# A nine-step scan on four engines: a bias and half of a multiply moved to ScalarE

## What is computed

```python
def mmnorm(x):
    return x / (jnp.max(jnp.abs(x), axis=-1, keepdims=True) + EPS)
def _scanner(y, x, freq_W, freq_b, out_W, out_b):
    z = jnp.concatenate([y, x], axis=-1)
    f = z @ freq_W + freq_b
    z = jnp.concatenate([jnp.sin(f), jnp.cos(f)], -1) @ out_W + out_b
    return mmnorm(z)
qv = x @ attn_W + attn_b
q, v = (qv[..., :c], qv[..., c:])
n = 1
while n < t:
    prev = jnp.concatenate([jnp.broadcast_to(identity, (b, n, c)), q[:, :t - n]], axis=1)
    q = _scanner(prev, q, freq_W, freq_b, out_W, out_b)
    n *= 2
Y = q * v
return Y @ proj_W + proj_b
```

## Time and profile before

| | |
|---|---|
| median of three runs | 2502.61 us (2501.95 to 2506.33) |
| profiled execution | 2498.18 us, span 2496.5 us |
| granted TensorE clock, mean | 0.983 of full |
| busy: TensorE, VectorE, ScalarE, GpSimd | 90%, 77%, 44%, 3% of the span |
| the scan's rounds | from about 66 to 475 us of the span |

### The profile page before, as it was taken

How to read it: one execution, slowest core, us unless ns; L and a number is a source line. 1 busy time by engine, 2 the same in 40 slices (tenths; PEclk the granted TensorE clock), 3 DMA queues, 4 the chain that set the end, 5 groups by cost and what they waited for, 6 DMA issues and landing times. The chain is left out here.

```text
span 2496.5 us, 37786 instructions
## 1 busy us (share of the span) xinstructions
PE 2254.8 (90%) x12609; PEld 1590.9 (64%) x12609; DVE 1923.8 (77%) x5516; ACT 1089.9 (44%) x1481; POOL 82.9 (3%) x135
## 2 busy tenths in 40 slices
PE   5999999899999998999879998998998999999997
PEld 4777777667666676676534454445675676666765
DVE  5768676689888889889845554555898898898897
ACT  1334343343443443544435554553444434434433
POOL 3200000000000000000000000000000000000000
PEclk9999999999999999999989998998999999999999
DMA  7000000000000000000000000000000000000000
GB/s 203 1 1 0 0 0 1 1 1 1 1 0 1 0 0 1 0 1 1 1 1 1 1 1 1 1 1 1 1 9 9 0 9 9 0 9 0 9 9 9
DMA packets 20782, 18.35 MB, mean 7 GB/s; under 512 B 6555, under 2 KB 19871, under 8 KB 20648
## 3 DMA queue, kind: packets, MB, share of 16 engines
q1 hardware_dynamic: 16106, 14.04, 1.9%
q10 hardware_dynamic: 4542, 2.78, 0.4%
HBM read 12.60 MB, written 4.19 MB: 7 GB/s over the span
## 5 line engine op out<-in xcount | busy, mean ns | idle before, releaser
L1355 ACT ACTIVATE f_E<-f_two 128x1024 f32<-128x1024 f32 x256 | 248.1, 1021 | 324.4 <-PE f_two L1237 324.4
L1091 DVE SCALAR_TENSOR_TENSOR f_E<-f_two,f_E 128x1024 f32<-128x1024 f32 x256 | 312.5, 1221 | 72.1 <-ACT f_E L1355 64.1
L1227 PE MATMUL f_acc<-ue,f_mid 128*128 128x256 f32 x1024 | 254.7, 395 | 11.7 <-DVE f_mid L1076 11.5
L1227 PEld LDWEIGHTS f_acc<-ue,f_mid 128*128 128x128 f32 x1024 | 192.9, 195 | 54.8 <-DVE f_mid L1076 18.6
L1142 PE MATMUL f_two<-f_hT,wg 128*128 128x512 f32 x768 | 211.4, 410 | 10.9 <-DVE f_mid L960 10.9
L1325 ACT ACTIVATE f_gate<-f_two,bg 128x512 f32<-128x512 f32 x128 | 88.1, 688 | 271.2 <-PE f_two L1142 270.9
L1142 PE MATMUL f_two<-f_hT,wu 128*128 128x512 f32 x768 | 200.0, 395 | 0.0
L1803 ACT ACTIVATE b_U<-b_two 128x768 f32<-128x768 f32 (+1 forms) x192 | 160.7, 886 | 69.2 <-PE b_two L1673 68.8
L1184 PE MATMUL f_acc<-wd,f_mid 128*128 128x256 f32 x768 | 188.1, 388 | 0.0
L1142 PE MATMUL f_two<-f_hT,deT 128*128 128x512 f32 x768 | 184.4, 395 | 0.0
L1142 PEld LDWEIGHTS f_two<-f_hT,wg 128*128 128x128 f32 x768 | 142.3, 188 | 49.8 <-DVE f_mid L960 15.3
(11 more groups left out here) (258 smaller groups left out, 3961.1 us busy)
## 6 DMA issues: line engine op xcount, KB each, us to landing
x<-in_L_attn_a_x SPq DMA_DIRECT2D x8, 512.0 KB, 7.4
out_x<-x SPq DMA_DIRECT2D x8, 512.0 KB, 2.9
de_rows<-in_L_ffn_down_embed ACTq DMA_DIRECT2D x1, 1024.0 KB, 5.8
wd<-in_L_ffn_Wd SPq DMA_DIRECT2D x1, 1024.0 KB, 10.1
ue<-in_L_ffn_up_embed SPq DMA_DIRECT2D x16, 64.0 KB, 5.8
whole_g<-in_L_ffn_Wg SPq DMA_DIRECT2D x1, 1024.0 KB, 6.3
whole_u<-in_L_ffn_Wu SPq DMA_DIRECT2D x1, 1024.0 KB, 8.8
ffq<-in_L_ffn_Wq ACTq DMA_DIRECT2D x4, 128.0 KB, 9.2
```

What stands on the lines that cost most here:

```text
L1091: dve.scalar_tensor_tensor(out=two_heads, in0=wide(turns, ("R", u))[:], scalar=PICKED_ABOVE, in1=two_heads, op0=ALU.is_gt, op1=ALU.mult).t ...
L1227: mm = pe.matmul(acc[:, j * C:(j + 1) * C], mixed[c % 2][:, j * P:(j + 1) * P], w.ue[:, c, :], start=False, stop=True, skip_group_check=True)
L1355: act.activation(E[:, c % 2, 2 * p:2 * p + 2].rearrange("p h t -> p (h t)"), wide(turns, ("S", u))[:], ACT.Exp).then_inc(S.act_read, 1)
```

## The change

It has two parts.

1. In steps 0 to 7, `gs` of lane 0 is written once and not twice by VectorE: 512 elements. ScalarE then copies the first place to the second, at the end of its step, behind the column writes, and sets `dup_ready`, for which TensorE's features of lane 0 wait in steps 1 to 8. Lane 1 is as before.
2. In steps 1 to 7 TensorE's `gain_bias(1, "gz")` is gone. ScalarE writes the bias into gb1 as 512 elements from `bias_gz`, a broadcast row of 128 columns, between whole0 and wave0. It waits there for lane 1's `gs_ready` (gb1 has been read) and sets `g1_begun`, for which TensorE waits between the zb product and the gb product of lane 1. Step 0 keeps TensorE's bias. The set-up gets one product and one ScalarE copy that make `bias_gz`.

```diff
+        bias_gz = ctx.enter_context(nc.sbuf_tensor("a_bias_gz", [P, P], F32))
...
                                 dve.wait_ge(S.g_psum, nth(i, NS, s + 1, l) + START)
-                                by = spread(spread(scale[l][:].rearrange("p j q -> p (j q)"), 2, 2), 3, NF)
-                                dve.tensor_tensor(gs[l][:], twice(gb[l]), by, ALU.mult).then_inc(S.gs_ready, 1)
+                                by = spread(scale[l][:].rearrange("p j q -> p (j q)"), 2, NF)
+                                if l == 0:
+                                    dve.tensor_tensor(gs[l][:, :, 0, :], gb[l][:].rearrange("p (q n) -> p q n", n=NF), by,
+                                                      ALU.mult).then_inc(S.gs_ready, 1)
+                                else:
+                                    dve.tensor_tensor(gs[l][:], twice(gb[l]), spread(by, 2, 2), ALU.mult
+                                                      ).then_inc(S.gs_ready, 1)
...
-                        pe.wait_ge(S.gs_ready, nth(i, NS, s, l) + START)
+                        if s > 0 and l == 0:
+                            pe.wait_ge(S.dup_ready, i * (NS - 1) + s + START)
+                        else:
+                            pe.wait_ge(S.gs_ready, nth(i, NS, s, l) + START)
...
                         if s < NS - 1:
+                            if s > 0 and l == 1:
+                                pe.wait_ge(S.g1_begun, i * (NS - 2) + s + START)
                             products(gb[l], P, [wave[l]], [w.gz[:]]).then_inc(S.g_psum, 1)
...
                         features(s, 1)
-                        if s < NS - 1:
-                            gain_bias(1, "gz")
...
-                pe.matmul(zb[0][:, 0:2], w.freq_bias[:], w.first_ones[:, T - 1:T + 1], start=True, stop=True
-                          ).then_inc(S.cols_psum, 1)
+                pe.matmul(zb[0][:, 0:2], w.freq_bias[:], w.first_ones[:, T - 1:T + 1], start=True, stop=True)
+                add_bias(pe, w, zb[1][:, 0:P], "gz", 2).then_inc(S.cols_psum, 1)
...
                             act.activation(whole[l][:], fb[l][:], ACT.Copy, bias=MAGIC).then_inc(S.whole_ready, 1)
+                            if l == 0 and 0 < s < NS - 1:
+                                act.wait_ge(S.gs_ready, nth(i, NS, s, 1) + START)
+                                act.activation(gb[1][:].rearrange("p (j n) -> p j n", n=P), spread(bias_gz[:], 1, TJ), ACT.Copy
+                                               ).then_inc(S.g1_begun, 1)
                             act.wait_ge(S.turns_ready, nth(i, NS, s, l) + START)
...
+                        if s < NS - 1:
+                            act.wait_ge(S.gs_ready, nth(i, NS, s + 1, 0) + START)
+                            act.activation(gs[0][:, :, 1, :], gs[0][:, :, 0, :], ACT.Copy).then_inc(S.dup_ready, 1)
...
-                act.activation(bias_cols[:], zb[0][:, 0:2], ACT.Copy).then_inc(S.cols_ready, 1)
+                act.activation(bias_cols[:], zb[0][:, 0:2], ACT.Copy)
+                act.activation(bias_gz[:], zb[1][:, 0:P], ACT.Copy).then_inc(S.cols_ready, 1)
```

More of the change, by code:

```diff
@@ L62, in __init__ @@
             "f_psum whole_ready turns_ready wave_ready peak_ready peak_eps scale_ready y_ready y_psum "
-            "proj_psum x_added g_psum f_begun cols_psum cols_ready "
+            "proj_psum x_added g_psum f_begun cols_psum cols_ready dup_ready g1_begun "
         ).split()]
@@ L68, in __init__ @@
          self.y_psum, self.proj_psum, self.x_added, self.g_psum,
-         self.f_begun, self.cols_psum, self.cols_ready) = self.all
+         self.f_begun, self.cols_psum, self.cols_ready,
+         self.dup_ready, self.g1_begun) = self.all
 class FfnSignals:
```

## The result

| | before | after | forecast |
|---|---|---|---|
| median of 15 runs each | 2501.95 us | 2487.3 us | 2491.8 (2488 to 2500) |
| lowest and highest | 2494.55, 2517.08 | 2478.9, 2494.77 | |
| ratio, 95% interval | | 0.9935 (0.9921 to 0.9950) | 0.9957 |
| profiled execution: time, span | 2498.18, 2496.5 | 2492.19, 2490.5 | 2487.4 |

The change is faster by 0.65%, 12.5 to 20 us by the interval, where 10.8 were forecast. The direction was right, the size too small, and the median lies 0.7 us under the range. Yet the two profiled executions are only 6 us apart. Both want an explanation. (The baseline moved little: the forecast started from a median of 2502.61 over three runs of before, and fifteen runs have 2501.95.)

A forecast was written before the change was run, and what follows sets the result against it. Two chains from gs1's end were taken to bound the scan step, TensorE's bias last (9.07 us, to become 8.56). Rounds of 2 x 3.4 + 2.4 + 1.8, less 0.2 set-up, save 10.8: 2491.8 us, range 2488 to 2500.

The forecast's parts named there:

- The bound: Scan step: two chains start at gs1's end; TensorE's bias sets zb0 at 9.07 us, the wave's chain would allow 8.81.
- points 1 to 3: Scan step: gb1's bias leaves TensorE; gs0 takes 0.69 us, 0.37 of 0.54 gets through; whole0 then sets zb0, 8.56.
- Point 4: ScalarE's gb1 bias write between whole0 and wave0: 0.60 us, up to 0.67, covered by turns0; beyond 0.70 it lengthens the step.
- Point 5: ScalarE's copy of gs0 behind the column writes: 0.63 us, covered by zb1 and gb1 with 0.5 to spare.
- Point 6: TensorE's wait for g1_begun between zb1 and gb1: already satisfied, taken as 0, at most 0.23 us.
- Point 7: Set-up's bias product and small ScalarE copy ahead of the first xT copies: 0.2 us for both, between 0 and 0.5.
- The sum: Scan: 3.4 us each in rounds 2 and 3, 2.4 in round 1, 1.8 in round 4, less 0.2 set-up: 10.8.
- step 5 gives some 0.3: Round 1 of the scan, around GpSimd's pass: step 5 saves some 0.3 us of the round's 2.4.
- the other three stages aren't touched and only shift: Stages outside the scan only move in time; the forecast gives them no saving of their own.
- Rivals B: Scan: ScalarE's write seen late or TensorE's g1_begun wait costs 0.2; 5 to 8 us saved, 2494.5 to 2497.6; chance 0.16.
- C: ScalarE's bias write takes about double, 1.2 to 1.36 us, so wave0 moves back; within 5 us, 2498 to 2507; chance 0.14.
- D: Same bias write ahead of wave0 costs more than 1.3 us; at 1.7 us, 10 us slower, 2513; chance 0.06.

The follow-up runs named there:

- experiment 2: Each part alone against before: only ScalarE's bias write, step 8.81 us, ratio 0.9955; only lane 0's halved multiply with ScalarE's copy, step 8.71 us, ratio 0.9965.
- experiments 2 to 5: Parts alone (0.9955, 0.9965); the change with set-up product later (0.9937), bias write doubled (1.0001), gs0's copy doubled (0.9959), lane 0's wave halved (0.9935, 0.9947); ratios to before.

## Why the prediction was wrong

By its steps:
- **The bound and points 1 to 3** (two chains from gs1's end; 0.26 for the bias; gs0 at 0.69, of which 0.37 gets through; whole0 next; 8.56) held to 0.02 in the trace, and each alone in experiment 2 (8.81 for 8.81, 8.71 for 8.70).
- **Point 4**, the bias write: 0.60, as taken, and free. The Trainium skill (ScalarE: Activation LUTs, What ACT_TABLE_LOAD costs) makes it 0.61; the trace agrees within 0.01. The prediction's remark that with 0.61 a later term would be 0.01 longer doesn't hold: the write would still end before turns0. That beyond about 0.7 every tenth goes into the step is shown by the double write (8.89 for 8.87). **Point 5**, the copy: 0.63, with half a microsecond to spare, shown by the double copy. **Point 6**: no gap between zb1's and gb1's loads. **Point 7**: the set-up's copy took 0.27 us. With the clock at 0.93 from 50 to 75 us the first zb0 came at 72.62 to 73.06 us in before and at 73.01 and 73.08 in the change, which neither shows nor excludes the 0.2 that I took.
- **The sum** was 1.0 us short in the scan (11.0 for 12.0), 0.7 of it in round 1, in the term "step 5 gives some 0.3". Behind GpSimd's pass VectorE is late and zb1 is done in time (at 119.14, where the second maximum starts at about 119.4), so nothing holds lane 1's maxima back. The rows, before and then after:

```profile
115.17 0.68 DVE L566 SCALAR_TENSOR_TENSOR a_turns<-a_whole,fb 128x512 f32<-128x512 f32 x1
...
115.76 1.45 DVE L574 TENSOR_REDUCE a_peak<-zb 128x2 f32<-128x512 f32 x2
...
117.78 1.22 DVE L584 TENSOR_TENSOR a_gs<-gb,a_scale 128x1024 f32<-128x1024 f32 x1
...
120.76 1.23 DVE L584 TENSOR_TENSOR a_gs<-gb,a_scale 128x1024 f32<-128x1024 f32 x1
```
```profile
115.76 0.68 DVE L568 SCALAR_TENSOR_TENSOR a_turns<-a_whole,fb 128x512 f32<-128x512 f32 x1
...
116.36 1.28 DVE L576 TENSOR_REDUCE a_peak<-zb 128x2 f32<-128x512 f32 x2
...
118.20 0.69 DVE L587 TENSOR_TENSOR a_gs<-gb,a_scale 128x512 f32<-128x512 f32 x1
118.81 1.28 DVE L576 TENSOR_REDUCE a_peak<-zb 128x2 f32<-128x512 f32 x2
...
120.65 1.22 DVE L590 TENSOR_TENSOR a_gs<-gb,a_scale 128x1024 f32<-128x1024 f32 x1
```

  From turns1 to gs1 it was 5.59 us and is 4.89: all of the 0.54 gets through here, and 0.16 that belong to this one trace of before. Its clock was at 0.50 from 110.0 to 116.8 us, and lane 0's maxima waited for slow zb products (1.45 for 1.28). In the other two traces of before the same stretch is 5.43 and 5.42, in the repeats of the change 4.89. So step 5 gives 0.54 and the 0.26 of the bias, 0.8 and not 0.3. Against those two traces the scan is 11.9 us shorter and the sum 0.9 short.
- **The step that failed** is "the other three stages aren't touched and only shift", and with it the range's "medians' own scatter of 1 to 2 us". The instructions only shift, but the time of these stages isn't fixed: 456 to 476 us in the linear attention, by the clock that it is granted. Single runs of one kernel have a standard deviation of 5.5 to 6.6 us, which makes some 4 us for a median of three and 2 for one of fifteen (an estimate from these deviations). A range 3.8 us deep below the forecast was too narrow for that.
- **What the runs show in its place.** Over all runs with a clock the means are 14.9 us apart: 12.0 in the scan, 1.8 that go with a mean clock 0.0010 (0.0006) higher, and 1.1 (0.3) at equal clock that was not found in any stage's trace. The cause of these last two terms stays open. Since the excess came up in all three batches, luck alone is a weak account of it; whether the change's timing earns the later stages a little clock, or gives about 1 us somewhere, or the fit leaves it over, no run tells. (The same remainder, gain at equal clock less gain in the scan, is 0.2 to 1.6 us for the kernels of experiments 2 to 5, without an order that I can see.) That the median came out 0.7 us below the range, and not just inside it, is smaller than the scatter.
- **Rivals B, C and D** are out: nothing of the additions on ScalarE was exposed.

## What to carry to other kernels

Work that moves to an engine with idle time is free only where another engine's instruction covers it: one more 0.6 us instruction cost next to nothing behind the column writes and 0.33 us a step between whole and wave. When two chains end together, price each against the other with the start of what they release; the name in the brackets is not enough. And get the scatter of the stages that a change doesn't touch from repeated runs before giving a range: here it was larger than the error of the whole step model. Where the scatter is that large, compare the changed stage's duration in the traces: it repeated to 0.2 us.

## What the runs showed of the hardware

- TensorE's granted clock varies from run to run of one program: means of 0.977 to 0.990 in the twelve runs of the change's first repeat, between which the times differ by 23 us (2497.5 and 2474.4). It falls to 0.50 in stretches of a few microseconds (54.0 to 60.8 us of the change's first trace, where TensorE loaded nothing for the 2.12 us before 54.53; 110.0 to 116.8 of before's first), and where they fall differs. One in the scan's set-up went with a first zb0 at 74.4 to 74.6 us and not 72.6 to 73.7, and the scan behind it repeated to 0.2 us.
- A ScalarE write to PSUM of 512 elements from a row of 128 that is read four times took 0.60 us, the same as whole's copy of 512 out of PSUM. A 512-element SBUF to SBUF copy with strided operands took 0.63, as the contiguous sine did.
- Two 256-element sines took 0.42 and 0.40, started 0.32 apart: splitting the wave cost 0.09 us of ScalarE time and won 0.22 us a step.
